# A two-layer transformer kernel on one core: the second weight transform of each attention round placed between state update and output of the first two chunks

## What is computed

```python
def _L0_ffn_ref(x, W1, W2, W3):
    up_gate = jnp.einsum('bsd,hd->bsh', x, W1)
    up_lin = jnp.einsum('bsd,hd->bsh', x, W3)
    hidden = jax.nn.silu(up_gate) * up_lin
    hidden = fwht(hidden)
    out = jnp.einsum('bsh,dh->bsd', hidden, W2)
    return out
...
x = _layernorm(x + _L0_attn_ref(x, ...), axis=-1)
x = _layernorm(x + _L0_ffn_ref(x, L0_ffn_W1, L0_ffn_W2, L0_ffn_W3), axis=-1)
x = _layernorm(x + _L1_attn_ref(x, ...), axis=-1)
x = _layernorm(x + _L1_ffn_ref(x, L1_ffn_w_gate_up, L1_ffn_w_down), axis=-1)
```

## Time and profile before

| what | us |
|---|---|
| median of 3 runs | 1906.67 |
| lowest and highest run | 1906.12, 1910.46 |
| the profiled execution's own time | 1907.46 |
| its span, first to last instruction | 1905.7 |
| PE busy | 1771.2 |
| DVE busy | 1339.0 |
| POOL busy | 1281.3 |
| ACT busy | 987.1 |

### The profile page before, as it was taken

How to read it: one execution, slowest core, us unless ns; L and a number is a source line. 1 busy time by engine, 2 the same in 40 slices (tenths; PEclk the granted TensorE clock), 3 DMA queues, 4 the chain that set the end, 5 groups by cost and what they waited for, 6 DMA issues and landing times. The chain is left out here.

```text
span 1905.7 us, 27715 instructions
## 1 busy us (share of the span) xinstructions
PE 1771.2 (93%) x9472; PEld 1136.7 (60%) x9472; DVE 1339.0 (70%) x1660; ACT 987.1 (52%) x1671; POOL 1281.3 (67%) x992
## 2 busy tenths in 40 slices
PE   7898998898999999889999899998999999999998
PEld 5666666577755565455555555554556555567886
DVE  2525344333259999899897999889999999994222
ACT  5344343566465656655556456555555555543212
POOL 4533444155449998798877898788889898883111
PEclk9999999899999999999999999999999999999999
DMA  7342332587668887688676887676778777874652
GB/s 243 129 144 73 122 110 92 183 298 272 240 217 278 290 294 264 215 299 276 209 251 226 276 278 253 236 238 231 248 256 278 253 254 254 279 261 155 209 190 98
DMA packets 159292, 427.37 MB, mean 224 GB/s; under 512 B 30992, under 2 KB 54160, under 8 KB 158768
## 3 DMA queue, kind: packets, MB, share of 16 engines
q1 hardware_dynamic: 159152, 425.60, 66.2%
HBM read 356.34 MB, written 69.21 MB: 223 GB/s over the span
## 5 line engine op out<-in xcount | busy, mean ns | idle before, releaser
L1627 ACT ACTIVATE decay<-delta_on_states,a_neg 128x512 f32<-128x512 f32 x512 | 353.9, 693 | 351.8 <-DVE h_states L1756 333.5
L1849 POOL TENSOR_TENSOR q_or_raw_or_h_times_c<-h_states,c_rep 128x512 f32<-128x512 f32 x293 | 382.9, 1318 | 63.1 <-DVE h_states L1756 38.0
L1849 POOL TENSOR_TENSOR h_times_c_rest<-h_states,c_rep 128x512 f32<-128x512 f32 x219 | 282.4, 1299 | 47.2 <-DVE h_states L1756 29.8
L1815 POOL TENSOR_TENSOR h_lo<-v_or_silu_in_h_lo,h_hi 128x512 fp32r<-128x512 f32 x128 | 167.0, 1305 | 207.4 <-ACT h_hi L1534 207.0
L1736 DVE TENSOR_TENSOR d_b<-du_spread,b_rep 128x512 f32<-128x512 f32 x384 | 256.4, 668 | 22.5 <-PE du_spread L1457 22.1
L1756 DVE TENSOR_TENSOR_SCAN h_states<-decay,h_last,d_b 128x512 f32<-128x512 f32 x192 | 245.5, 1279 | 12.7 <-ACT decay L1627 5.9
L1457 PE MATMUL du_spread<-stack,selectors 96*128 96x512 bf16 x512 | 201.3, 393 | 49.2 <-DVE d_b L1736 34.2
L1756 DVE TENSOR_TENSOR_SCAN h_states<-decay,d_b 128x512 f32<-128x512 f32 x192 | 233.9, 1218 | 17.5 <-ACT decay L1627 11.3
L111 PE MATMUL y_or_aux<-h_hi,w 128*128 128x512 f32 x468 | 222.2, 475 | 6.6 <-POOL h_lo L1815 4.3
L112 PE MATMUL y_or_aux<-h_lo,w 128*128 128x512 f32 x468 | 184.1, 393 | 0.0
L113 PE MATMUL y_or_aux<-h_hi,w 128*128 128x512 f32 x468 | 183.5, 392 | 0.0
(11 more groups left out here) (251 smaller groups left out, 4205.4 us busy)
## 6 DMA issues: line engine op xcount, KB each, us to landing
delta_on_states<-delta SPq DMA_DIRECT2D x256, 512.0 KB, 5.4
w<-w_split SPq DMA_DIRECT2D x112, 512.0 KB, 4.3
attn_w_hi_or_x_hi_w<-w_split SPq DMA_DIRECT2D x112, 512.0 KB, 4.3
attn_w_lo_or_x_lo_w<-w_split SPq DMA_DIRECT2D x112, 512.0 KB, 4.3
w_split<-w_presplit_hi_lo SPq DMA_DIRECT2D x32, 512.0 KB, 3.3
w_presplit_hi_lo<-in_w13b SPq DMA_DIRECT2D x32, 256.0 KB, 3.8
w_split<-attn_w_hi_or_x_hi_w SPq DMA_DIRECT2D x8, 1024.0 KB, 6.8
w_split<-attn_w_lo_or_x_lo_w SPq DMA_DIRECT2D x8, 1024.0 KB, 7.0
```

Source lines behind the costliest of these rows:

```text
L1627: act.activation(da[:, s % ND], dring[:, s % NR], ACT.Exp, scale=a[:, column(s):column(s) + 1]).then_inc(s_da, 1)
L1815: pool.tensor_tensor(hl[:, idx % RH], sg[:, idx % RH], hh[:, idx % RH].bitcast(F32), ALU.subtract).then_inc(s_hl, 1)
L1849: pool.tensor_tensor(hc[s % NC_], hs[:, s % NH], crep[:, tile_of(s // SPO) % 2], ALU.mult).then_inc(s_hc, 1)
```

## The change

The two halves of `had1` leave their place between the gate and `kT` on PE. In rounds 0 to 2 the first half is done in chunk 0, between `state_update` and `from_chunk`, and the second half at the same place in chunk 1. In round 3 both are done in chunk 0. In the item lists `had1` becomes the last item. ACT takes the halves at the start of the next round, after the high part of x. That high part now waits for two items fewer, so that it still starts behind the last `wo` (or `kT`). SP's and POOL's programs are unchanged.

```diff
-        FIRST = (["q"] * KD + ["had0"] * 2 + ["k"] * KD + ["v"] * CPT + ["gate"] * KD + ["had1"] * 2
-                 + ["kT"] * CPT)
+        FIRST = (["q"] * KD + ["had0"] * 2 + ["k"] * KD + ["v"] * CPT + ["gate"] * KD
+                 + ["kT"] * CPT + ["had1"] * 2)
...
-                    def transform(i):
+                    def transform(i, half):
 
-                        pe.wait_ge(s_bf, BF * (2 * t + i) + BF)
-                        for half in range(2):
-                            out = bank(f"had{i}", half)
+                        if half == 0:
+                            pe.wait_ge(s_bf, BF * (2 * t + i) + BF)
+                        out = bank(f"had{i}", half)
...
-                    transform(1)
...
                     for c in range(CPT):
                         from_state(c)
                         state_update(c)
+                        if c == 0:
+                            transform(1, 0)
+                        if c == (1 if t + 1 < NT else 0):
+                            transform(1, 1)
                         from_chunk(c)
...
                     if not rd.first and not rd.tail:
-                        act.wait_ge(s_pj, rd.base)
+                        act.wait_ge(s_pj, rd.base - 2)
                         act.copy(xh[:, :, :], x[:, :, tok(t)]).then_inc(s_xh, 1)
+                    if not rd.first:
+                        take_transformed(ROUNDS[rd.prev], 1)
...
-                    take_transformed(1)
                     blocks_high(beside_outputs(t))
```

More of the change, by code:

```diff
@@ L194, in by_piece @@
             return (whole, count) if k == KD - 1 else (piece, k + 1)
-        FIRST = (["q"] * KD + ["had0"] * 2 + ["k"] * KD + ["v"] * CPT + ["gate"] * KD + ["had1"] * 2
-                 + ["kT"] * CPT)
+        FIRST = (["q"] * KD + ["had0"] * 2 + ["k"] * KD + ["v"] * CPT + ["gate"] * KD
+                 + ["kT"] * CPT + ["had1"] * 2)
         SECOND = (["q"] * KD + ["had0"] * 2 + ["norm"] * KD + ["k"] * KD + ["v"] * CPT + ["gate"] * KD
-                  + ["had1"] * 2 + ["kT"] * CPT + ["wo"] * KD)
+                  + ["kT"] * CPT + ["wo"] * KD + ["had1"] * 2)
         NEXT = (["mp"] + ["q"] * 2 + ["mb"] + ["q"] * 2 + ["had0"] * 2 + ["vp"] + ["norm"] * KD + ["vb"] + ["k"] * KD
-                + ["v"] * CPT + ["gate"] * KD + ["had1"] * 2 + ["kT"] * CPT + ["wo"] * KD)
+                + ["v"] * CPT + ["gate"] * KD + ["kT"] * CPT + ["wo"] * KD + ["had1"] * 2)
         TAIL = ["norm"] * KD + ["wo"] * KD
@@ L399, in outputs @@
                             project("wo", 3, m, onh, onl, (lambda k: [(s_ol, KD * rd.prev + k + 1)]) if m == 0 else None)
-                    def transform(i):
-                        pe.wait_ge(s_bf, BF * (2 * t + i) + BF)
-                        for half in range(2):
-                            out = bank(f"had{i}", half)
-                            rows = had[0][:, half * (NC // 2):(half + 1) * (NC // 2), :]
-                            pe.matmul(out, const[:, C_HAD:C_HAD + P],
-                                      rows.rearrange("p c d -> p (c d)")).then_inc(s_pj, 1)
+                    def transform(i, half):
+                        if half == 0:
+                            pe.wait_ge(s_bf, BF * (2 * t + i) + BF)
+                        out = bank(f"had{i}", half)
+                        rows = had[0][:, half * (NC // 2):(half + 1) * (NC // 2), :]
+                        pe.matmul(out, const[:, C_HAD:C_HAD + P],
+                                  rows.rearrange("p c d -> p (c d)")).then_inc(s_pj, 1)
                     def gate_partial_sums():
@@ L496, in body @@
                         pe.wait_ge(s_const, 16)
-                    transform(0)
+                    transform(0, 0)
+                    transform(0, 1)
                     if rd.norms_x:
```

10 lines of the change are left out of this document (5 added, 5 removed).

## The result

The changed kernel takes 1932.1 us (median of 5 runs, 1924.68 to 1932.36), the kernel before 1906.67; the ratio is 1.0125 (95% interval 1.0107 to 1.0143). So it is 25.4 us slower. The forecast was 1918.5, so +11.8: the right direction with less than half the size, and the time lies 6.6 us above the range's upper end. The profiled execution took 1932.34 with a span of 1930.6.

The account below looks back on a forecast made before the run. The prediction took PE, busy 1771.2 us, to bound the kernel. Gains, queue, shared access, clock, round 3's chunk and tail summed as -2.8 + 9.8 + 2.1 + 1.7 + 0.7 + 0.3 = +11.8: 1918.5 us, range 1904.5 to 1925.5.

Parts of the forecast that it names:

- the queue: SP's later loads delay POOL's butterflies; PE stalls before the first transform of rounds 1 to 3: 4.6 + 2.6 + 2.6 = 9.8 us.
- the first link: From SP's first load to the landing of the first block's store, which frees a buffer: 8.4 us.
- the second: Second link, from the first of the next blocks' loads to the end of POOL's third low part: 7.9 us.
- the shared access: A butterfly beside DVE's decayed q takes longer: 2.1 us in round 1, nothing in rounds 2 and 3, at most 2.1 each.
- The step for round 0 and 1: Shift up to round 1's gate: round 0's gain, round 1's stall, shared access and clock, -1.86 + 4.6 + 2.1 + 1.7 = +6.5 us.
- the gain of round 0: In round 0 the first transposes start where the transform started, 1.86 us sooner.
- Both halves in one chunk of round 3: Two halves, 1.98 us together, in a gap of 1.23 put 0.7 us on PE's path.
- In rounds 1 to 3 less comes back: Before the transposes DVE is late next, so PE gains only 0.27, 0.34 and 0.34 us there.
- the clock term: PE at half clock once, behind round 1's stall: 1.7 us; none behind the stalls of rounds 2 and 3, at most 1.7 each.
- rival (d): Longest chain, with clock and shared access in all three rounds' stalls: +21.2 us, 1928; chance 0.12.
- The tail: After round 3, PE waits for the feed-forward's first weights, loaded late by SP: 0.3 us, up to 1.5.
- (a): Rival: SP's blocks land sooner, stalls are short, without clock or shared access: 1906 to 1909; chance 0.22.

Follow-up runs that it names:

- e1: The changed kernel, with SP storing and loading its blocks ahead of its wait for the second transform: 1908.8 us, beside 1907.8 for the kernel before.
- e4: The move made in round 0 alone, rounds 1 to 3 with the second transform in its old place: 1911.6 us, beside 1907.8 for the kernel before.
- e9b: e1 plus two products nobody reads on PE ahead of the third transposes in rounds 1 to 3: 1905.0 us, beside 1907.8 for the kernel before.
- e2: The changed kernel with 5, 3 and 2 unread products on PE before the first transform of rounds 1 to 3: 1930.7 us.
- e13: The kernel before with 20 unread products on PE ahead of round 3's first transform, a pure delay: 1925.2 us, beside 1907.9 without.
- e14: The kernel before with 14 unread products on PE ahead of round 3's first transform, a pure delay: 1920.4 us, beside 1907.9 without.
- e5: The changed kernel measured again, with nothing altered: 1935.3 us, beside 1907.5 for the kernel before.
- e10b: The changed kernel with unread products before the first transform and third transposes (rounds 1 to 3), and DVE's decayed q waiting for butterflies in rounds 1 and 2: 1921.2 us.
- e3: The changed kernel, with DVE waiting in rounds 1 and 2 for POOL's butterflies before making the decayed q: 1924.9 us, beside 1907.8 before.
- e8: The kernel before, with SP's blocks ahead of its wait for the second transform, as in e1: 1910.1 us, beside 1907.5 without.

## Why the prediction was right in its chain and wrong in its size

**Right: the direction, the queue and every link of the chain.** SP started at 69.82 (69.7 forecast), the first link took 8.2 us (8.4), the second 8.2 (7.9). The three stalls add to 12.3, against 9.8 for the queue and 2.1 for the shared access, 11.9. e1 shows by itself that the stalls come through SP's queue. The step for round 0 and 1 gave +6.5 and the profile +6.8, e4 +6.1.

**Right: the gain of round 0 and the chunks.** 1.64 where 1.86 was forecast, or 1.86 with the 0.22 of lateness taken off, and waits for `probs` of 0.20 as worked out. Both halves in one chunk of round 3 cost +0.6 (0.7 forecast).

**Wrong: "In rounds 1 to 3 less comes back".** This step gave -0.27 and -0.34 a round; measured +1.0, +0.6, and some +0.6 in round 3 (17.82 at the gate, 18.37 behind `wo`). The step read the right rows and took DVE as next, but it looked at when DVE ends only, and not at what PE does until then: it idles 2.98 us where the transform had been, and the clock is halved for the next 3.4. e9b shows it by putting work back there: with it the rounds give -0.4 and -0.4, near the forecast.

**Wrong: the clock term, "1.7 once".** The prediction had the row for it and applied it to the longest stall alone, with at most 1.7 for the others. In the changed kernel the lower clock came behind two stalls for 6.8 us each, and behind the three idle times before the transposes. The half-clock time up to the trunk is 30.7 us against 6.8. By the prices that the experiments gave (2.0 for 6.8 us behind a stall, e2; about 1.2 for 3.4 us behind the transposes, e9b, e13 and e14) the five come to some 7.6 us, an estimate from single profiles, where 1.7 stood in the sum. This is the term that was mis-sized most.

**Wrong: the shared access "at nothing" in rounds 2 and 3.** It came in round 2 of the first profile (last butterfly 3.31 us, stall 4.20), and in rounds 2 and 3 of e5. The bound of 2.1 each stood in the prediction, and rival (d), "the stall repeats in full", with 0.12. Its 1928 was nearest to what came, but it counted the clock at 1.7 a stall and had no idle time before the transposes.

From the gate of round 1 to that of round 2 the forecast was +2.3 and the profile +7.7. With the stall at 4.20 in place of 2.6 that leaves 3.8: 1.3 from the gate to the next start, and 2.5 behind, mostly the half clock of 6.8 us. Summed over the phase: 11.8 forecast, 20.4 measured, so 8.6 more: 4.1 in round 2's stall with its clock, 4.1 between the gate and the next start in rounds 1 to 3 (1.3, 1.0, 1.8), 0.5 in small rests. Of round 3's 1.8, 0.9 is the idle time and its half clock (the shift grows by 0.55 from the gate to the first scores, with -0.34 forecast), and 0.2 is ACT's squares behind the casts, as in e10b. The rest, 0.8, is a pause of PE in the middle of chunk 2's scores:

```profile
346.48 0.37 PE L430 MATMUL scores<-q_or_raw_or_h_times_c,kT 32*128 32x128 f32 x1 [0.49 <-issue]
```

The scores' record before it began at 345.72, and "issue" says that PE waited for nothing that the profile shows. The same pause is in e1 (at 330.9) and in round 2 of e9b (at 244.3), not in before. What causes it stays open.

**Wrong, and not explained: nothing for the trunk.** Its part was +4.5, +2.2 and -0.6 in the three profiles; e13 and e14 speak against a cost of the late start by itself, and the cause stays open.

**The tail** cost +0.5 behind the squares (0.3 forecast). SP there, in the changed kernel:

```profile
340.06 0.53 SPq L292 DMA_DIRECT2D w_hadamard<-had_b  x1
340.63 3.71 SPq L305 DMA_DIRECT2D w_split<-w_presplit_hi_lo  x3
347.08 1.56 SPq L300 DMA_DIRECT2D w_presplit_hi_lo<-in_w13b  x2
348.69 0.43 SPq L324 DMA_DIRECT2D had_a<-in_w13a  x1
```

SP took 8.6 us from the store to the first weights' load, where the prediction had 6.5, since the next block's load followed the first store after 6.45 us (3.46 before). PE's lateness by then hid most of it; e10b shows it at 3.17.

One slip in the prediction's rivals: the 1906 to 1909 of (a) is counted from the profiled execution's 1907.46, the times of the others from the median of 1906.67. From the median (a) is 1905.6 to 1907.8, and nothing else changes.

## What to carry to other kernels

When work is taken out of an engine's way and its successor on another engine is late anyway, the engine idles in that place, and it may lose more by a lower clock behind the idle time than it gains, as here in rounds 1 to 3: look at what it will do in the freed time, not only at when the next result comes. When a product is moved later, follow every queue whose waits name it, and move what doesn't depend on it ahead of that wait; here two lines of SP's program were worth 23 us. Price companions of a stall (clock, shared access) for every stall that can have them, since their timing is decided by tenths of a microsecond.

## What was not expected of the hardware

Two products of no use in an idle time of 3 us made the kernel 3.7 us faster by the medians (e1 to e9b), as PEclk there was 1.00 in place of 0.50. A stretch at the lower clock was 3.4 us long in some places and 6.8 in others, and the idle time ahead doesn't tell which: 6.8 behind 6.11 and 4.20 us (the changed kernel), 3.4 behind 4.00 (e3) and 4.13 (e5), and 3.4 behind 1.40 (e8, e13, e14), where most such rounds show none. DVE's and POOL's subtractions of two inputs in SBUF, side by side, took 5.66 us for four and 4.64 for three, where apart they take 2.50 and 3.8. And the same program's attention phase varied by 13 us between three profiles, in part because a third of a microsecond decides whether a butterfly or the decayed q goes first.
